# Scatters of tokens' rows paced by a count of attention's steps on TensorE

## What is computed

```python
xn = _layernorm(x)
x = x + gated_linear_attention(xn) + moe(xn)
# gated_linear_attention: q, k, v, decays gk; S = S*exp(g) + k v^T; o = q S; norm, gate, @ Wo
# moe: top-2 of 8 experts by xn @ Wr; y = W2(silu(xn W1) * (xn W3)); weighted sum of the two
```

## Time and profile before

| | |
|---|---|
| median of 3 runs | 3989.31 us (3987.63 to 4007.27) |
| the profiled execution, its own time | 4015.07 us |
| its span, first to last instruction | 4013.3 us |
| busy PE / DVE / ACT / POOL | 89% / 63% / 44% / 28% |
| mean granted clock of TensorE | 0.927 |
| layer 0's attention and experts | about 90 to 980 us of the span |

### The profile page before, as it was taken

One profiled execution on the slowest core, in us unless ns is written; L12 is line 12 of the kernel. 1 busy time (PEld: TensorE's weight loads), 2 busy tenths in 40 slices (PEclk: granted clock), 3 DMA queues, 4 the chain that ended last, 5 costly groups with the idle time before them and its releaser, 6 DMA issues.

```text
span 4013.3 us, 47937 instructions
## 1 busy us (share of the span) xinstructions
PE 3588.1 (89%) x16596; PEld 2098.4 (52%) x16596; DVE 2540.2 (63%) x6419; ACT 1763.4 (44%) x3258; POOL 1139.9 (28%) x1174
## 2 busy tenths in 40 slices
PE   8299999958898989898887998999799999999998
PEld 6167777734554545445445666777543333433332
DVE  4153333454788888888866555443467777777784
ACT  2043443313234433343334444444236666666667
POOL 0601111250354555555542222222221111111111
PEclk7599999979899999998988999999899999999999
DMA  4325565421466666666651000000111011111100
GB/s 159 136 87 174 190 203 199 135 68 67 116 192 181 191 204 189 196 196 202 188 162 42 0 1 1 0 1 1 37 24 23 21 30 27 29 34 30 32 18 22
DMA packets 121763, 382.13 MB, mean 95 GB/s; under 512 B 28240, under 2 KB 56032, under 8 KB 111536
## 3 DMA queue, kind: packets, MB, share of 16 engines
q0 software_dynamic: 57328, 301.90, 24.0%
q1 hardware_dynamic: 63104, 75.05, 6.6%
q10 hardware_dynamic: 1088, 2.10, 0.2%
HBM read 322.32 MB, written 31.20 MB: 88 GB/s over the span
## 4 chain that ended last, share of the span: by engine, by line
PE 62%; DVE 23%; issue 5%; ACT 5%; POOL 2%; DMA 1%; another core or an unknown queue 1%; POOLq 0%; SPq 0%; ACTq 0%; DVEq 0%
PE ps L184 49%; PE ps L2505 5%; DVE pm L2653 4%; PE ps L1445 2%; DVE gathB L1622 2%; DVE mi L1564 2%; DVE hacc L1606 2%; DVE ps L2656 2%; ACT P L2786 1%; POOL gathA L1761 1%; PE ps L2017 1%; DVE mx L1560 1%; DMA gathA<-in_tab,idx 1%; DVE tm L1522 1%
## 5 line engine op out<-in xcount | busy, mean ns | idle before, releaser
L2786 ACT ACTIVATE P<-ps 128x512 f32<-128x512 f32 (+3 forms) x1280 | 586.6, 547 | 219.8 <-PE ps L184 217.5
L2653 DVE TENSOR_REDUCE pm<-ps 128x1 f32<-128x512 f32 x768 | 484.1, 682 | 118.7 <-PE ps L184 118.6
L1761 POOL DMA_INDIRECT gathB<-in_tab,idx x256 | 283.1, 1106 | 404.4 <-PE ps L1445 334.2
L184 PE MATMUL ps<-QS,KS 49*128 49x512 f32 (+3 forms) x1280 | 335.4, 425 | 16.2 <-DVE pm L2653 12.7
L1761 POOL DMA_INDIRECT gathA<-in_tab,idx x256 | 277.1, 1082 | 234.8 <-DVE gte L1578 157.1
L184 PE MATMUL ps<-KS,QS 48*128 48x512 f32 (+3 forms) x1280 | 311.6, 433 | 15.4 <-DVE pm L2656 5.9
L2505 PE MATMUL ps<-P,Va 128*32 128x512 f32 (+3 forms) x2560 | 312.5, 562 | 5.7 <-POOL P L2843 2.9
L2843 POOL TENSOR_SCALAR_AFFINE_SELECT P<-P 128x256 f32<-128x256 f32 x256 | 103.3, 406 | 721.1 <-ACT P L2786 720.3
L184 PEld LDWEIGHTS ps<-QS,KS 49*128 49x128 f32 x1280 | 159.4, 192 | 227.4 <-DVE pm L2653 82.3
L2656 DVE CUSTOM_DVE_ANT_0 ps<-ps,past 128x128 f32<-128x128 f32 (+3 forms) x512 | 239.5, 513 | 30.7 <-PE ps L184 28.8
L184 PEld LDWEIGHTS ps<-KS,QS 48*128 48x128 f32 x1280 | 147.0, 193 | 212.4 <-DVE pm L2653 65.5
(11 more groups left out here) (377 smaller groups left out, 7093.1 us busy)
## 6 DMA issues: line engine op xcount, KB each, us to landing
xs_sorted<-zero SPq DMA_DIRECT2D x1, 9088.0 KB, 33.6
xs<-xs_sorted SPq DMA_DIRECT2D x71, 128.0 KB
ys_sorted<-ys SPq DMA_DIRECT2D x71, 128.0 KB, 1.7
KS<-hi SPq DMA_DIRECT2D x256, 32.0 KB, 2.0
QS<-hi SPq DMA_DIRECT2D x256, 32.0 KB, 2.0
gathA<-in_tab,idx POOLq DMA_INDIRECT x256
gathB<-in_tab,idx POOLq DMA_INDIRECT x256
KS<-lo SPq DMA_DIRECT2D x128, 32.0 KB, 2.0
```

Of the source, the lines that this page charges most:

```text
L184: m = pe.matmul(out, w, x, start=start and i == 0, stop=stop and i == len(pairs) - 1, skip_group_check=True)
L1761: pool.indirect_dma_start(out=(GA, GB)[half][:, h, :], out_offset=None, in_=d[f"tab{half}"], in_offset=bass.IndirectOffsetOnAxis(ap=idx[t ...
L2653: v = dve.tensor_reduce(m, p, AX.X, ALU.max)
L2786: act.activation(P_[:, hh, off:BW], psx.tile("s2", j, n, kt, pr, hh)[:, off:BW], ACT.Exp).then_inc(*psx.emptied(MN.act, "s2", j, n, kt, pr ...
```

## The change

Before every second group c of the scatters, so before every four of them, POOL waits until `AT.pe` has reached 3(c/2) - 1: 2 before c = 2, then 5, 8, 11, 14, 17 before c = 12, and so on to 44 before c = 30. Nothing else is changed. The first four scatters wait as before, for `posu`.

```diff
                 for c in range(NC):
+                    if c % 2 == 0 and c > 0:
+
+                        pool.wait_ge(AT.pe.sem, 3 * (c // 2) - 1)
                     for s in range(2):
                         pool.indirect_dma_start(out=XS, out_offset=bass.IndirectOffsetOnAxis(ap=posu[:, s, c:c + 1], axis=0),
                                                 in_=xtok[c], in_offset=None, bounds_check=TILES * 128 - 1,
```

## The result

The changed kernel takes 3953.55 us (median of 4 runs, 3935.68 to 3963.98) where the kernel before takes 3988.47 us (3987.02 to 4007.27). The ratio is 0.9897, with a 95% interval of 0.987 to 0.9923, so the change saves 31 to 52 us, 35 us between the medians. The forecast was 3964 us, 25 us faster.

The account below looks back on a forecast made before the run. TensorE was taken to bound layer 0 except from about 113 to 192 us, where scatters run. Gain 58 us, less 20 for attention still held, less 13 for the profile, is 25: 3989.3 - 25 = 3964 us, range 3933 to 3993.

Parts of the forecast that it names:

- The place and the first stop: POOL first stops at the 25th scatter, c = 12, 127.8 us; TensorE's late-known semaphore updates come through about 128.5 us.
- The share that attention loses: Share f of indirect-DMA time lost to attention in layer 0; gain 58 - 74 f, taken as 0.27, costing 20 us.
- Without further hindrance: After POOL's first stop no update is held again: experts start at 195.6 instead of 253.4 us, a gain of 58 us.
- One reading: In layer 0, finished TensorE ticks become known 34 to 53 us late, three almost together when indirect DMAs end.
- It passes on: From 248 to 780 us TensorE is busy 97%, so the experts' earlier start moves everything behind it up in full.
- the correction for the profile: Profiled run 25.8 us above the median; half, 13 us, charged to layer 0's idle stretch and taken off the gain.
- the hole: Layer 0, about 113 to 192 us: TensorE, DVE and ACT mostly idle during scatters; 62 us of waits in the chain.
- That the hole isn't the scatters' or is the profiler's: Rival: layer 0's idle stretch has another cause or exists only in profiles; time stays 3989 us, plus 4 at most; chance 0.15.
- attention is held as much within short bursts: Rival: layer 0's attention held nearly as much within bursts of four scatters; 3969 to 4005 us, middle 3985; chance 0.21.
- The slower case: Rival: experts come too late, every burst freezing attention and TensorE's clock staying at half; 4023 us; chance 0.08.
- f = 1: Every burst of four scatters freezes attention; experts start at about 270 us, 16 us later than before.
- f = 0: Scatters hold attention no further after POOL's first stop; experts start at 195.6 us, weights in time or nearly so.

Follow-up runs that it names:

- one memset: No waits on attention; GpSimd does one small memset, waited for, before every four scatters, against the kernel before: 3940.45 us, ratio 0.9856.
- one wait: The changed kernel with only the wait for tick 17 before c = 12 kept of its 15 waits: 3985.15 us, ratio 0.9971 to the kernel before.
- one pair of scatters: The kernel before with only the first two of the 64 scatters, so the experts compute on zeros: 3916.7 us, ratio 0.9787.
- two memsets: No waits on attention; GpSimd does two small memsets, each waited for, before every four scatters, against the kernel before: 3953.12 us, ratio 0.9877.
- half of the scatters: The kernel before with 32 scatters, one for each group of tokens instead of two: 3962.21 us in one run.

## Why the prediction was right

**The place and the first stop** were right to the instruction: POOL stops at the 25th scatter, the earlier waits cost nothing, and the held updates come through at 131.0 us (forecast 128.5).

**The share that attention loses** was taken as f = 0.27, 20 us. Without further hindrance the experts would have started at 195.6 us + 2.5 us for the later release; they start at 213.0 us, 14.9 us later, and the three waits of 2.96, 2.96 and 9.40 us, 15.3 us together, account for that. That is f = 14.9 / 74 = 0.20. The first line 672 was forecast at 253.4 - 38 = 215.4 us. The size was near, but the picture behind f was only half right, and that part was luck. I spread the loss over all bursts of four. In fact only four of the 15 waits stop POOL; where several in a row are already met, the bursts join to unbroken runs, of 8 scatters from 138.29 us and of 20 from 161.83 us. The waits start 11.2 and 15.4 us into these runs (149.47 and 177.22 us). The largest, 9.40 us, stands behind the last tick that is waited for, 44, which ends at 177.7 us (forecast 170.4), so none of the 15 waits could have ended it.

**One reading was wrong.** The prediction says that three ticks become known almost together when the indirect DMAs end. In the kernel before they became known one by one, at 155.01, 166.21 and 171.12 us, while POOL went on issuing until 178.84 us. Only in the changed kernel, after POOL's stop, did they come almost together: ACT takes `o` at 130.98 us and `v` at 131.47 us, DVE takes `kt` at 132.26 us.

**It passes on**: 253.41 - 212.96 = 40.4 us at the first line 672, 43.4 us at the first normalisation of layer 1 (its line 299 starts at 997.93 instead of 1041.37 us), 51.1 us at the end. Of the 10.7 us behind the first line 672, 2.2 us come from the gathers' unknown waits (18.9 to 16.7 us) and 7.7 us appear in later layers that the change doesn't touch. I put them down to the scatter between two executions, which isn't shown. Between the medians the gain is 35 us.

**The step that was mis-sized** is the correction for the profile. I charged half of the 25.8 us between profile and median to the hole. Nine later kernels have more than one execution, one of each profiled. In six the profiled one lies among the others. In two it lies above them, by 1.1 us (the changed kernel) and 9.9 us (one memset), and in one below, by 0.5 us (one wait). The kernel before alone ranges from 3974.57 to 4020.12 us over all runs and chips. So nothing shows a cost of profiling, and the 25.8 us lie within the spread of the kernel before; that its held waits differ from run to run would explain the spread, and isn't shown. Without the 13 us the forecast would have been 3951 us; measured are 3953.55 us. With them, the 25 us forecast lie below the measured 31 to 52 us.

**The rivals.** That the hole isn't the scatters' or is the profiler's fell with one pair of scatters: 79 us faster. That attention is held as much within short bursts fell with the 15.3 us above. The slower case didn't come, but half of its mechanism is real: the experts' tokens do come too late once attention runs free, 26.6 us with two memsets. I had it under f = 1, and wrote at f = 0 that the weights are in time or nearly so, from scatters that end at 179.9 us; with the breaks they end at 191.3 us, and attention is there at 172.7 us.

**The Trainium skill's rule** (SBUF — State Buffer, "Who interferes with whom": "DMA never contends with a compute engine") holds here for data: plain DMAs at 259 GB/s don't slow TensorE. It doesn't cover what decides this case, that an update of TensorE is known 70.7 us late beside 14 GB/s of indirect DMAs.

What stays open is what in an unbroken run of indirect DMAs holds the updates. The runs show that a break early enough prevents a hold, but not that any break ends one: with half of the scatters 2.3 us without an issue ended nothing, and nor did the same 2.3 us in the kernel before (178.84 to 181.16 us, update of `a` at 191.42 us). Whether the memset or the time matters isn't settled either. The changed kernel's stops of 1.64 and 1.80 us are breaks without an instruction, and after each the next hold starts 11 to 15 us later, as at the start of a run. That speaks for the time, but no kernel had such a break before every four scatters.

## What to carry to other kernels

When several engines idle together in a profile and go on at one update of a semaphore, ask who was issuing meanwhile, not who was computing. Try to break long runs of indirect DMAs on GpSimd, here every four, with a small instruction that is waited for. Here it cost 1 us each and depended on no other engine. Then look at what the freed engine meets next: here the consumer's own data were late, and the order written by hand had to move with it.

## What the runs showed of the hardware

- In an unbroken run of indirect DMAs on GpSimd, issued every 1.28 us, updates of TensorE's semaphores arrive late. The first are late by a few us, about 10 to 15 us into the run. Then `o` of chunk 0 is known 42.1 us after its end in the kernel before, 17.6 us in the changed one and 70.7 us with scatters of 16 rows. It happens at 14 as at 101 GB/s, with 16 rows as with 128.
- Breaks of 1.0 or 1.25 us before every four indirect DMAs kept all updates on time; a break of 2.3 us during a hold didn't end it.
- 64 plain DMAs of the same 8.4 MB, from GpSimd's or SyncE's queue, hold nothing, at 192 to 267 GB/s.
- An indirect scatter of 128 rows occupies GpSimd for 0.98 us and one of 16 rows for 0.85 us, each with 0.30 us behind; the plain DMA of 128 rows takes 0.54 us.
- TensorE's granted clock fell to 0.50 (1.2 GHz) in the hole and was 1.00 throughout from 96 to 172 us in the kernel with two memsets, where TensorE was busy 70.15 of 76 us. Behind the hole it was still 0.50 from 155 to 192 us and 0.81 from 192 to 208 us, so the restart is slow too.
